# The output projection of an attention kernel turned round: results as the moving side, and the sum turned back by TensorE

## What is computed

```python
q = (pre_q @ Wq + bq).reshape(b, ql, H, D_Q)
k = (pre_k @ Wk + bk).reshape(b, kl, H, D_Q)
v = (pre_k @ Wv + bv).reshape(b, kl, H, D_Q)
scores = jnp.einsum('bqhd,bkhd->bhqk', q, k) / jnp.sqrt(jnp.float32(D_Q))
attn = jax.nn.softmax(scores, axis=-1)
ctx = jnp.einsum('bhqk,bkhd->bqhd', attn, v).reshape(b, ql, H * D_Q)
x = pre_q + (ctx @ Wo + bo)
mu = jnp.mean(x, axis=-1, keepdims=True)
var = jnp.mean(jnp.square(x - mu), axis=-1, keepdims=True)
return (x - mu) * jax.lax.rsqrt(var + EPS) * gamma + beta
```

## Time and profile before

| | |
|---|---|
| three runs | 874.96, 875.16, 880.12 us; median 875.16 us |
| profiled execution | 878.73 us, of which the span 876.9 us |
| busy in the span: TensorE matmuls, weight loads | 98%, 70% |
| VectorE, ScalarE, POOL | 91%, 86%, 55% |
| TensorE's granted clock, mean | 0.994 of full |
| 12 tiles of an even window, 13 of an odd one | together about 103 us |

### The profile page before, as it was taken

How to read it: one execution, slowest core, us unless ns; L and a number is a source line. 1 busy time by engine, 2 the same in 40 slices (tenths; PEclk the granted TensorE clock), 3 DMA queues, 4 the chain that set the end, 5 groups by cost and what they waited for, 6 DMA issues and landing times.

```text
span 876.9 us, 19574 instructions
## 1 busy us (share of the span) xinstructions
PE 855.9 (98%) x7312; PEld 617.0 (70%) x7312; DVE 796.3 (91%) x997; ACT 757.5 (86%) x1060; POOL 479.7 (55%) x515
## 2 busy tenths in 40 slices
PE   7999999999999999999999999999999999999996
PEld 6577776766777777776677677677767767777675
DVE  4799989899998999989899998999999899999984
ACT  4899898988889898898888889898888989988983
POOL 4053883459746574664637466473755657376210
PEclk9999999999999999999999999999999999999999
DMA  9699999999999999999999999999999999999995
GB/s 232 128 222 196 195 196 182 221 209 206 195 214 209 217 210 229 207 213 216 213 212 213 217 204 219 212 218 215 213 225 220 208 221 211 214 195 208 209 182 123
DMA packets 683041, 180.79 MB, mean 206 GB/s; under 512 B 654596, under 2 KB 682052, under 8 KB 682948
## 3 DMA queue, kind: packets, MB, share of 16 engines
q1 hardware_dynamic: 681332, 178.48, 104.0%
q10 hardware_dynamic: 1344, 0.53, 0.2%
q0 software_dynamic: 272, 0.53, 0.2%
HBM read 15.35 MB, written 0.82 MB: 18 GB/s over the span
## 4 chain that ended last, share of the span: by engine, by line
PE 46%; DVE 27%; ACT 12%; issue 9%; DMA 4%; SPq 1%; ACTq 0%; DVEq 0%; POOLq 0%; POOL 0%
PE ps L660 21%; PE ps L621 20%; DVE p_lo L919 11%; DVE nmax L904 10%; ACT p L1065 6%; ACT p_hi L1073 3%; DMA pt_hi<-p_hi 3%; PE ps L479 2%; DVE rsum L910 1%; ACT unused L1030 1%; PE ps L486 1%; DVE rinv L912 1%; ACT c_hi L1012 1%; PE ps L471 1%; DMA ct_hi<-c_hi 1%
## 5 line engine op out<-in xcount | busy, mean ns | idle before, releaser
L919 DVE SCALAR_TENSOR_TENSOR p_lo<-p,rinv,p_hi 128x1444 f16<-128x1444 f32 x200 | 362.5, 1812 | 2.7 <-ACT p_hi L1073 2.1
L904 DVE TENSOR_REDUCE nmax<-ps 128x1 f32<-128x1446 f32 x200 | 329.9, 1650 | 12.6 <-PE ps L621 12.2
L1073 ACT ACTIVATE p_hi<-p,rinv 128x1444 f16<-128x1444 f32 x200 | 300.1, 1501 | 47.1 <-DVE rinv L912 46.2
L1065 ACT ACTIVATE p<-ps,nmax 128x1446 f32<-128x1446 f32 x200 | 292.0, 1460 | 30.1 <-DVE nmax L904 28.5
L660 PE MATMUL ps<-pt_hi,c_hi 128*128 128x256 f16 (+1 forms) x1232 | 253.4, 261 | 5.9 <-DMA pt_hi<-p_hi 3.6
L660 PE MATMUL ps<-pt_hi,c_lo 128*128 128x256 f16 (+1 forms) x1232 | 253.3, 261 | 0.0
L621 PE MATMUL ps<-ct_hi,g_hi 128*128 128x482 f16 (+3 forms) x624 | 155.6, 368 | 2.9 <-DMA ct_hi<-c_hi 2.9
L621 PE MATMUL ps<-ct_lo,g_hi 128*128 128x482 f16 (+3 forms) x624 | 155.5, 367 | 0.0
L621 PE MATMUL ps<-ct_hi,g_lo 128*128 128x482 f16 (+3 forms) x624 | 155.5, 367 | 0.0
L660 PEld LDWEIGHTS ps<-pt_hi,c_hi 128*128 128x128 f16 x1232 | 114.3, 98 | 42.8 <-issue 8.8
L660 PE MATMUL ps<-pt_lo,c_hi 128*128 128x256 f16 (+1 forms) x1232 | 138.7, 261 | 0.0
(11 more groups left out here) (134 smaller groups left out, 801.2 us busy)
## 6 DMA issues: line engine op xcount, KB each, us to landing
c_raw<-in_ctx_dram SPq DMA_DIRECT2D x32, 256.0 KB
pt_hi<-p_hi SPq DMA_TRANSPOSE x200, 3.5
pt_lo<-p_lo SPq DMA_TRANSPOSE x200, 3.7
c_raw<-in_ctx_dram SPq DMA_DIRECT2D x16, 192.0 KB
c_raw<-in_ctx_dram SPq DMA_DIRECT2D x48, 18.0 KB
out_dram<-late_sb SPq DMA_DIRECT2D x16, 50.0 KB
x_sb<-in_x_dram SPq DMA_DIRECT2D x1, 600.0 KB
o_t<-in_L_xattn_Wq_dram SPq DMA_DIRECT2D x2, 256.0 KB, 4.4
```

The lines of the kernel that those rows point to most:

```text
L904: dve.tensor_reduce(nmax[:, n % RING:n % RING + 1], ps[:, bank:bank + 3, 0:KEYW], AX.XY, ALU.max, negate=True).then_inc(s_nm, 1)
L919: dve.scalar_tensor_tensor(out=p_lo[:, n % LOS, 0:KL], in0=p32[:, n % P32S, 0:KL], scalar=rinv[:, i:i + 1], in1=p_hi[:, par, 0:KL], op0=AL ...
L1065: act.activation(p32[:, n % P32S, :].rearrange("p (k w) -> p k w", w=KEYW), ps[:, bank:bank + 3, 0:KEYW], ACT.Exp, bias=nmax[:, i:i + 1], ...
L1073: act.activation(p_hi[:, par, 0:KL], p32[:, n % P32S, 0:KL], ACT.Copy, scale=rinv[:, i:i + 1]).then_inc(s_hi, 1)
```

## The change

For the 13 batches in f16 parts (2 to 14) the two operands of the output projection are exchanged: m16 (128 columns) is loaded as weights, and the 100 columns of o16 move. The sum then stands as 128 rows (output feature) by 100 columns (query). In tile 9 ScalarE copies it with the output's scale to the new buffer out_t; in tile 10 TensorE turns it back, with the identity as the moving side, to 100 rows by 128 columns elsewhere in JOB_BANK, and VectorE's take_rows, now in tile 10, adds the residual without a scale. The spreading of the context's magnitude and context_scale go from tile 10 to 11. The parts of JOB_BANK are dealt out anew, and one wait (s_ma) is added once, before the first query projection that follows the spreading of m's maximum.

```diff
-    TOP_AT = 10
-    TOP_AT_FIRST = 11
+    BACK_AT = 10
+    TOP_AT = 11
...
+        out_t = sb("out_t", [P, 2, QL])
...
-                        mm = pe.matmul(bank[0:QL, 0:D], o16[:, i, rows], m16[:, h, j, :], start=(h == 0 and i == j),
+                        mm = pe.matmul(bank[:, 0:QL], m16[:, h, j, :], o16[:, i, rows], start=(h == 0 and i == j),
...
+                    if g == 0 and b == window(MTOP_AT)[0] + 2:
+                        pe.wait_ge(s_ma, 1)
...
-                if r == (TOP_AT if w else TOP_AT_FIRST) and w + 2 < B:
+                if r == BACK_AT and w > 0 and in_parts(w - 1):
+                    pe.wait_ge(s_of, w - FIRST_PARTS)
+                    pe.transpose(bank[0:QL, P:2 * P], out_t[:, (w - 1) % 2, :], ident[:, :]).then_inc(s_bk, 1)
+                if r == TOP_AT and w + 2 < B:
...
             def take_rows(b):
                 par = b % 2
-                dve.wait_ge(s_fin, b + 1)
+                if in_parts(b):
+                    dve.wait_ge(s_bk, b - FIRST_PARTS + 1)
+                    at = P
+                else:
+                    dve.wait_ge(s_fin, b + 1)
+                    at = 0
...
-                if in_parts(b):
-                    dve.wait_ge(s_fu, b - FIRST_PARTS + 1)
-                    dve.scalar_tensor_tensor(out=z[:, par, :], in0=ps[0:QL, JOB_BANK, 0:D], scalar=fin_un[0:QL, par:par + 1],
-                                             in1=x_sb[:, b, :], op0=ALU.mult, op1=ALU.add).then_inc(s_z, 1)
-                else:
-                    dve.tensor_tensor(z[:, par, :], ps[0:QL, JOB_BANK, 0:D], x_sb[:, b, :], ALU.add).then_inc(s_z, 1)
+                dve.tensor_tensor(z[:, par, :], ps[0:QL, JOB_BANK, at:at + D], x_sb[:, b, :], ALU.add).then_inc(s_z, 1)
...
-                if r == ROWS_AT and w > 0:
+                if w > 0 and r == (BACK_AT if in_parts(w - 1) else ROWS_AT):
                     take_rows(w - 1)
...
-                if r == (TOP_AT if w else TOP_AT_FIRST) and w + 2 < B:
+                if r == TOP_AT and w + 2 < B:
                     context_scale(w + 2, ps[:, JOB_BANK, :])
...
+            def columns_out(b):
+                act.wait_ge(s_fin, b + 1)
+                act.wait_ge(s_fu, b - FIRST_PARTS + 1)
+                act.activation(out_t[:, b % 2, :], ps[:, JOB_BANK, 0:QL], ACT.Copy,
+                               scale=fin_un[:, b % 2:b % 2 + 1]).then_inc(s_of, 1)
...
+                if r == ROWS_AT and w > 0 and in_parts(w - 1):
+                    columns_out(w - 1)
```

More of the change, by code:

```diff
@@ L293, in cross_attention_kernel @@
         s_fin = sem("output_projected")
+        s_of = sem("projected_columns_copied")
+        s_bk = sem("projected_rows_turned_back")
         s_z = sem("residual_added")
@@ L544, in spread_context_max @@
                 pe.wait_ge(s_part_id, 2)
-                pe.matmul(bank[:, 0:P], spread(c_max[:, NT + 1:NT + 2]), ident_part[:, min(b, 1), :], start=True, stop=True).then_inc(s_top, 1)
+                pe.matmul(bank[:, 2 * P:3 * P], spread(c_max[:, NT + 1:NT + 2]), ident_part[:, min(b, 1), :], start=True, stop=True).then_inc(s_top, 1)
             def spread_ax_max(bank):
@@ L549, in spread_ax_max @@
                 for i in range(2):
-                    mm = pe.matmul(bank[:, (1 + i) * P:(2 + i) * P], spread(ax_max[:, i:i + 1]), ident[:, :], start=True, stop=True)
+                    mm = pe.matmul(bank[:, i * P:(1 + i) * P], spread(ax_max[:, i:i + 1]), ident[:, :], start=True, stop=True)
                 mm.then_inc(s_axt, 1)
@@ L728, in job @@
                         pe.wait_ge(s_mc, 1)
-                        pe.matmul(bank[:, P:2 * P], spread(m_max[:, :]), ident[:, :], start=True, stop=True).then_inc(s_mt, 1)
+                        pe.matmul(bank[:, 3 * P:4 * P], spread(m_max[:, :]), ident[:, :], start=True, stop=True).then_inc(s_mt, 1)
                     spread_context_max(bank, w + 2)
@@ L846, in context_scale @@
                 un = unscale[:, b % UNSCALES:b % UNSCALES + 1]
-                dve.tensor_reduce(un, bank[:, 0:P], AX.X, ALU.max).then_inc(s_us, 1)
+                dve.tensor_reduce(un, bank[:, 2 * P:3 * P], AX.X, ALU.max).then_inc(s_us, 1)
                 dve.wait_ge(s_us, b + 1)
@@ L885, in parts_scale @@
                 dve.wait_ge(s_axt, 1)
-                dve.tensor_reduce(ax_top[:, :], split(ps[:, JOB_BANK, P:], 2, P), AX.X, ALU.max).then_inc(s_axa, 1)
+                dve.tensor_reduce(ax_top[:, :], split(ps[:, JOB_BANK, :], 2, P), AX.X, ALU.max).then_inc(s_axa, 1)
                 dve.wait_ge(s_axa, 1)
@@ L894, in m_parts_scale @@
                 dve.wait_ge(s_mt, 1)
-                dve.tensor_reduce(m_top[:, :], ps[:, JOB_BANK, P:2 * P], AX.X, ALU.max).then_inc(s_ma, 1)
+                dve.tensor_reduce(m_top[:, :], ps[:, JOB_BANK, 3 * P:4 * P], AX.X, ALU.max).then_inc(s_ma, 1)
                 dve.wait_ge(s_ma, 1)
```

## The result

| | before | changed |
|---|---|---|
| median of ten runs | 877.66 us (874.96 to 880.12) | 881.72 us (879.24 to 885.2) |
| ratio | | 1.0040, 95% interval 1.0022 to 1.0057 |
| profiled execution, its span | 878.73, 876.9 us | 879.24, 877.4 us |

The change costs some 4 us, 0.4%: less than the one per cent at which the prediction drew its line, but clear of zero. The forecast was +2.0 us on 875.16, which is 877.2, with a range of 871.5 to 881; 881.72 lies just above it. The difference is about twice the forecast one, and the kernel before, of which three runs had been shown, has medians of 876.6 to 877.9 us in all sets measured since.

A forecast was written before the change was run, and what follows sets the result against it. VectorE and ScalarE were taken to set the pace in windows 3 to 13, TensorE barely keeping up. Terms +1.9 + 0.6 - 0.5 = +2.0 us on 875.16 gave 877.2, predicted as 877, range 871.5 to 881.

The forecast's parts named there:

- windows 3 to 13: VectorE/ScalarE's chain in five even and six odd windows grows by 0.2 + 1.7 = +1.9 us.
- POOL's later work: POOL's row finishing, next scales and subtraction come one tile later and meet other p_lo passes: 0 to 2.0, taken as +0.6 us.
- the ends: Windows 14 and 15 gain about 0.5 us each from the matmuls; window 15 gives 0.83 back at tile 10; put at -0.5.
- context_scale from 10 to 11 (in window 0 it stays): VectorE's context_scale moves a tile later, adding 0.51 us to the step from tile 11 to 12.
- Even windows: Steps at tiles 9 to 12 of 3.65, 4.36 and 4.04 us plus 0.34 for a slow p_lo: +0.03 us.
- slow p_lo: VectorE's p_lo pass beside POOL's subtraction takes 2.15 us instead of 1.71; 0.34 us counted from tile 11 to 12.
- Odd windows: Four steps from tile 9, with ScalarE's new copy and the O_BANK copy exposed, take 15.94 us instead of 15.66: +0.28.
- TensorE's time turns into waits: TensorE's net saving of 4.8 us does not shorten the kernel but becomes idle time before transposes and weighing.
- Rival A: TensorE is the bound, so the time falls by the net 4.8 us, to 870.4; chance 0.11.
- rival B: The move shortens the VectorE/ScalarE chain: copy hides, slow p_lo falls away; -3.3 us, to 871.9; chance 0.15.
- Rival C: The turning back stalls TensorE into the chain in 11 windows: +3.3 us on the forecast sum, 880.5; chance 0.11.
- Rival D: The change costs and gives nothing, +-0.5 of 875.2 us, odd windows hiding the copy; within the forecast's 0.63 chance.

The follow-up runs named there:

- e10: Changed kernel with the spread of the maxima back at tile 10 in window 2 alone; ratio to the kernel before 0.9999.
- e11: Kernel before with the spread of the maxima moved to tile 11 in window 2 alone, plus the s_ma wait; ratio 1.0050.
- e2: Kernel before with take_rows moved to tile 10 and context_scale to tile 11, plus the s_ma wait; 884.38 us, ratio 1.0084.
- e3: Kernel before with take_rows in tile 10, context_scale in tile 11, and ScalarE's new copy in tile 9, which nobody reads; 882.8 us, ratio 1.0067.
- e1: Kernel before with only the operands of the 624 f16 output projection matmuls exchanged, sum not turned back, output wrong; 876.14 us, ratio 0.9977.
- e4: Kernel before with take_rows put ahead of row_inverse in tile 9, in VectorE's idle time; 874.39 us, ratio 0.9966.
- e6: Changed kernel without the 13 transposes; VectorE reads the columns as they stand, behind ScalarE's copy; 882.31 us, ratio 1.0054.
- e8: All of the change a tile earlier, turning back ahead of the weighing, take_rows ahead of row_inverse, Wo awaited by group; 910.01 us, ratio 1.0363.
- e9: As e8, but TensorE turns the columns back behind the weighing of tile 9, not ahead of it; 876.84 us, ratio 1.0007.
- e7: Kernel before with take_rows ahead of row_inverse in tile 9 and TensorE's wait for Wo taken group by group; 874.49 us, ratio 0.9955.
- after_again: The changed kernel itself, measured a second time against the kernel before; ratio 1.0047.
- e5: Changed kernel with TensorE waiting for the two-part Wo group by group, not for all four groups at once; 875.55 us, ratio 0.9987.

## Why the prediction was right or wrong

**The step that failed, a missing term: +4.** The prediction's sum had three pieces: windows 3 to 13, POOL's later work, and the ends. What a later spread does once, between windows 2 and 3, stood in it at nothing, without a reason. Its list of what moves said "context_scale from 10 to 11 (in window 0 it stays)" and costed the 0.51 us of VectorE. It did not follow what else is issued in that place. In window 2 the same job carries Wo's maximum, behind which stand ScalarE's four copies, POOL's four splits and TensorE's first f16 projection. All stand in the code; and the trace had the sign of it in a row that carried a term of the sum. The matmul group in the earlier trace rows ends in "2.0 <-issue 2.0": a single wait of 2.0 us of the line that was being replaced, not followed up, because the view of waits began at 230 us and this one ends at 213.7. A wait of 2 us means that the thing waited for is already late. The change started POOL's chain a tile (4.0 us) later and ended it 2.9 us later; the wait became 4.9, and the stretch from tile 6 of window 3 takes 32.8 to 33.0 us against 28.3 to 28.5 without the longer wait. Moving that one job back gives all of it back (e10), moving it alone costs all of it (e11).

**The windows: right in kind, wrong in size.** Even windows: forecast +0.03, measured -0.37 (window 8, 49.63 for 50.00), of which 0.3 is the slow p_lo that now falls into the next window's first step; so -0.07. Odd windows: forecast +0.28, measured +0.40 (window 13), which is the same 0.3 and +0.1. A pair thus costs +0.03 instead of +0.31. The term that failed is the odd window's steps: 3.92, 4.36 and 3.62 were summed, and the trace shows 3.88, 4.30 and 3.55 in window 9:

```profile
539.96 1.45 ACT L1073 ACTIVATE p<-ps,nmax 128x1446 f32<-128x1446 f32 x1
...
543.32 0.32 ACT L1094 ACTIVATE out_t<-ps,fin_un 128x100 f32<-128x100 f32 x1
543.56 0.38 ACT L1102 ACTIVATE o_t<-ps 128x256 f32<-128x256 f32 x1
543.84 1.46 ACT L1073 ACTIVATE p<-ps,nmax 128x1446 f32<-128x1446 f32 x1
...
548.14 1.47 ACT L1073 ACTIVATE p<-ps,nmax 128x1446 f32<-128x1446 f32 x1 [0.83 <-DVE nmax L912]
...
552.18 1.47 ACT L1073 ACTIVATE p<-ps,nmax 128x1446 f32<-128x1446 f32 x1
...
555.73 1.47 ACT L1073 ACTIVATE p<-ps,nmax 128x1446 f32<-128x1446 f32 x1
```

Each is off by 0.04 to 0.07, and that times three in six windows is 1.0 of the 1.9 us. Without the new matmul form the same windows cost about what was forecast (568.31 and 568.16 in e2 and e3, 1.3 to 2.5 us above the 565.9 to 566.9 of kernels without the move).

**"TensorE's time turns into waits": right.** In the old layout the columns leave windows 8 and 13 unchanged to 0.01 us (e1). Rival A, 4.8 us faster, has fallen. One reservation: with the block a tile later the relief seems to matter in odd windows, 53.92 without the columns (e3), 53.58 with them. The step from tile 9 to 10 is 3.85 for 4.04 us there; the copy of O_BANK falls right behind the new copy, and TensorE had been the later of the two (its 0.31 us in e2). Of the next step's 0.13 us some 0.06 is the cheaper sum (0.29 for 0.35), which both kinds of window have.

**The view behind that reading.** The Trainium skill, "Perfetto Trace Analysis", section "Identifying the Most-Contended Engine", would have matmul busy time discounted, and MFU (the share of the peak arithmetic) and the weight loads' share taken; the prediction took the second of these. Window 8 agrees: 0.52 us less matmul work left its 50.00 us as they were (e1, 49.99), while 0.8 us of VectorE's work moved into a gap took 0.5 off (e4, 49.50). The totals say less, -2.0 us for 6.8 of matmul work and -3.0 for some 12 of VectorE's (0.8 in 15 windows), since the odd windows give part back; ScalarE's copies waited 14.2 us for TensorE in e4, 10.4 before.

**POOL's later work: +0.6 forecast, none found.** The slow p_lo was met as before, one tile later. The half of rival B that had it fall away did not come about.

**Rival C, the turning back stalls TensorE into the chain.** ScalarE's waits for TensorE did not grow (10.2 us for 10.4), and without the transposes the time is no less (e6), though these waits then fall to 2.1 us. As the change places it, C is excluded beyond 2 us. But the mechanism is real: with everything a tile earlier, the turning back ahead of the weighing cost 32 us (e8), and behind it 0.6 (e9).

**Rival D, nothing lost and nothing gained.** With window 2 restored this is what is left (-0.1). Its reason, odd windows that hide the new copy behind a wait for TensorE, is seen in e2 and e3 (4.05 and 4.04 us from tile 9 to 10 of window 13, without the copy and with it). In the changed kernel that step is 3.85 to 3.88 us, where the prediction had 3.92.

**The ends: -0.5 forecast, -0.1 measured.** From tile 0 of window 15 to the last exponentials 47.49 became 47.67 us: four steps gained 0.14 each from the matmuls, and the block at tile 10 gave 0.77 back (3.53 to 4.30), where 0.83 was forecast. Window 14 gained 0.3 (48.90 to 48.59). The prediction's own working, twice 0.5 less 0.83, is -0.2, and was right; the -0.5 that it wrote down does not follow from it.

**The sum again.** Forecast 1.9 + 0.6 - 0.5 = +2.0. Measured: windows and POOL about 0, ends -0.1, window 3 +4. Two errors of opposite sign, and a result near the forecast for a reason that was not the forecast one: with window 2 restored the forecast's +2.0 lies outside the interval of -1.3 to +1.2. And the base was off: the three runs shown had a median of 875.16, all later sets of 10 to 26 gave 876.6 to 877.9; taking the same offset for both kernels carried that error into the predicted time.

## What to carry to other kernels

When an edit moves a place in a loop, list everything that is ever issued at that place, in the first rounds too: one-time work hangs on the same constants as the steady work, and a stall that happens once costs as much as 0.3 us in each of 13 windows. Read the waits over the whole span before choosing a stretch, and look up each wait that stands in the row of the very line that the change replaces: its producer is already late. A semaphore wait for all parts of something that arrives in parts can cost next to nothing (here, 0 to 1 us, e7 against e4) until the schedule shifts; waiting part by part is a safer habit.

## What the runs showed of the hardware

**TensorE's clock after a short stop.** The same wait before window 3's first f16 projection is 1.9 to 4.9 us long in these kernels. The view of windows, stretches of 4 us, the last three columns granted clock, DMA share and GB/s; of before, of the changed kernel, of e4 and of e1:

```profile
213.00:217.00 4.00, 3.26 (x20) 1.73 (x21) 2.94 (x4) 3.82 (x8) 3.84 (x5) 0.76 1.18 212
```

```profile
213.00:217.00 4.00, 2.92 (x17) 1.74 (x18) 0.32 (x2) 3.08 (x5) 3.84 (x6) 0.59 1.16 256
```

```profile
213.00:217.00 4.00, 2.63 (x23) 1.69 (x24) 3.39 (x3) 4.00 (x7) 3.84 (x5) 1.00 1.17 210
```

```profile
213.00:217.00 4.00, 2.39 (x22) 1.45 (x23) 3.48 (x2) 3.99 (x7) 3.84 (x4) 1.00 1.18 204
```

After 4.88 us of idling part of the stretch ran at the lower level, 1.2 GHz: three score matmuls took 1.41 us where they take 0.78. After 2.02 us in the profiled execution of before the clock fell as well (0.76); after 1.86 us in e4, 2.01 in e1 and 2.12 in e10, it stayed at 1.00, and the step of the exponentials took 3.98 us instead of 4.74. So the length of the stop alone does not tell, near 2 us, whether the lower level follows. It is also a part of why the stretch from tile 6 of window 3 is 29.96 us in the profiled execution of before and 28.3 to 28.5 in e1 and e4, so that held against that one execution the change seemed to lose 2.9 us there and not the 4.4 that it loses against e1, e4 and e10. By these stretches, as an estimate, 2.9 of the 4.4 us are the longer wait and 1.5 the lower clock, in the changed kernel as in that execution of before.

**The same POOL instruction at two durations.** The last subtraction of the Wo groups took 1.16 us in the kernel before and 2.44 in the changed one (the last rows of POOL's timelines above), with the same operands. The traces repeat it: 2.44 us in the seven traces with the spread of Wo's maximum at tile 11 (changed, after_again, e2, e3, e5, e6, e11), 1.15 or 1.16 in the seven with it at tile 10. What stood beside it on VectorE differs just so: a pass of p_lo in each of the first seven, a row maximum in each of the others. Here the changed kernel, then the one before:

```profile
211.22 1.75 DVE L927 SCALAR_TENSOR_TENSOR p_lo<-p,rinv,p_hi 128x1444 f16<-128x1444 f32 x1
```

```profile
212.02 1.65 DVE L904 TENSOR_REDUCE nmax<-ps 128x1 f32<-128x1446 f32 x1
```

That p_lo is the cause was not tried. These 1.28 us stand on the path that TensorE waits for: in the changed kernel they are part of its 4.88.
